# A two-layer transformer on one core: moving work between stages, normalisations to ScalarE, and a later load

## The chip, the cores and the metric

The kernel runs on one core of a Trainium2 chip. The core has five engines that run side by side, each through its own list of instructions in order: TensorE (PE, matrix products into PSUM), VectorE (DVE), ScalarE (ACT), GpSimd (POOL) and SyncE (SP, which here only issues DMA transfers). An instruction waits at the head of its engine's list until semaphores reach given values, and all that stands behind it waits with it. The metric is the time of one execution on the device in microseconds; lower is better.

## The reference

`x` is one sequence of T = 2048 tokens with C = 256 features. Two layers follow one another, each attention and then an FFN, each with normalisation before and behind it:

```python
x = x + LN(attn0(LN(x)))      # low-rank projections, rotary halves of the heads
x = x + LN(ffn(LN(x)))
x = x + LN(attn1(LN(x)))      # one qkv projection
x = x + LN(ffn(LN(x)))

# attention 0, H = 16 heads of 16 (8 plain + 8 rotary features)
c_q  = LN85(x @ W_d_q.T + b) * g + b2         # 85 features
q    = c_q @ W_u_q.T + b                      # second half of each head rotated
c_kv = x @ W_d_kv.T + b                       # 128 features, LN128 as kv_n, and 8 for k_r
k_n, v = kv_n @ W_u_kv.T + b                  # k = [k_n, rotated k_r]
# both attentions
y = softmax(causal(q @ k.T * scale)) @ v      # T x T scores for each head
out = y @ W_o.T + b_o
# both FFNs, 256 -> 1024 -> 256, int8 weights with a scale for each column
silu(h @ w_gate * s_gate) * (h @ w_up * s_up) @ w_down * s_down
```

LN is (x - mean) / sqrt(var + eps) over the features.

## The kernel before

Tokens lie in 16 tiles of 128, or in 4 chunks of 512 (`NCH` = 4, `TPC` = 4 tiles in a chunk). One program holds both layers one behind the other. Each layer `L` has four stages.

**Projections.** Queries and keys are made in 16 units (`UNITS`), each one product of 128 rows by 512 tokens (`unit_products`, TensorE). Each unit is then split into three bf16 parts, so that scores can be made from bf16 products: `split_hi` (ScalarE, L519), `unit_rem` (VectorE, L681), `split_mid` (ScalarE, L524), `split_lo` (GpSimd, L423). SyncE stores the parts to HBM (L354), and reads them back as stacks, in which a head's parts stand in the order that the scores want: `load_queries` (L329) and `load_keys` (L340) take three DMAs each, of 3, 2 and 1 copies of 16 rows with 4 KB in a row. `load_stacks(g, c)` does both for head group `g` (4 heads) and chunk `c`; there is room for two groups, `g % 2`. Values are made in 8 steps (`v_products`, TensorE; `v_value`, VectorE, L688). In layer 0 the units need a down-projection first: `chunk_down` (VectorE, L735 to L744), a root on ScalarE (L549), `chunk_z` (VectorE, L754, eight normalising operations a chunk), a transpose (L961, L962), and L552 on ScalarE. The plans `PE_BEFORE`, `DVE_BEFORE` and `ACT_BEFORE` say before which unit each chunk of that is done.

**Attention.** 16 steps, each one head group and one chunk of queries, in the order `STEP_ORDER`: group 0 with chunks 0, 1, 2, 3 (steps 0 to 3), then group 1 with chunks 3, 2, 1, 0 (steps 4 to 7), and so on. The string `TURNS` sets by hand in which order TensorE takes S (a 128x512 or shorter piece of scores; VectorE takes its maximum, L780 or, on the diagonal, L782), M (the maxima become rows), T (transposed scores; ScalarE takes the exponential, L569), V (probabilities times values) and Y (end of a step). The other engines follow the same order. TensorE waits before the first S that uses a stack until it has landed (`stack_in`). Thirty-three pieces of scores stand before the first T, and the first T of step 2 is the T with number 24; the first S of step 4 is turn 221 and needs the stacks of group 1 for chunks 3 and 0.

The loads of group 1 are issued by SyncE in the order of chunks 0, 1, 2, 3, behind this wait (`s.t_filled` counts the T products; `T_N` is their number in a layer):

```python
                sp.wait_ge(s.t_filled, L * T_N + 1)
                for c in range(NCH):
                    load_stacks(1, c)
                for n, (g, Q) in enumerate(STEPS):
```

Before the first S of a layer, TensorE waits until all 16 units' `unit_rem` and all 8 values are done (`p.rem`, `p.v_sb`).

**Output projection.** 16 products with W_o, bias (VectorE, L817), normalisation (statistics L627 and L630, root L488 on ScalarE, `normalize_branch` L640 on VectorE, added to `x` by GpSimd, L428), and the normalisation of the sum for the FFN (`normalize_residual`, L664), transposed on TensorE (L882) and moved by `move_transposed` (L503) and `low_parts` (L672).

**FFN.** 32 iterations `u` = (chunk `c`, block `i` of 128 hidden features): eight gate and up products, silu (ScalarE, L603), the product of both (VectorE, L847), a low part (VectorE L850, GpSimd L472), and, one iteration late, twelve down products. The last of a chunk is taken out by VectorE (L838) and normalised as above for chunk `c - 1` while chunk `c` runs. Layer 1's transposes, units and values stand behind the last iteration of layer 0's FFN.

## Time and profile before

| | us |
|---|---|
| median of 3 executions | 1278.7 (1278.65 to 1279.92) |
| the profiled execution | 1275.28, of it 1273.5 in the span |
| projections, layer 0 | 0 to 86.0 |
| attention, layer 0 | 86.0 to 506.3 |
| output projection, layer 0 | 506.3 to 534.5 |
| FFN, layer 0 | 534.5 to 645.0 |
| projections and first scores, layer 1 | 645.0 to 723.5 |
| attention, layer 1, from its first T | 723.5 to 1126.6 |
| output projection, layer 1 | 1126.6 to 1154.8 |
| FFN, layer 1 | 1154.8 to 1263.9 |

TensorE is busy for 1164.4 us (91% of the span), VectorE for 1049.9, ScalarE for 720.6, GpSimd for 334.7. The rows of a window give the stretch, its length, the busy time and the number of instructions of each engine, the TensorE clock that was granted as a share of full speed, and the DMA engines' busy share and rate. The rows of a timeline give start, duration (of a run of like instructions), engine, line, what is written and read, the count, and in brackets how long the engine was idle before and what released it. A product of float32 stands in the trace as two records (pieces) of TensorE.

### The profile page before, as it was taken

The numbers are of one execution on the slowest core, as the hardware profiler recorded it, in microseconds if no ns is written. First come the engines' busy times: TensorE is split into PE (matmuls) and PEld (weight loads), VectorE is DVE, ScalarE is ACT, GpSimd is POOL, SyncE is SP. The second block draws the span as 40 slices with busy tenths as digits, with TensorE's granted clock in tenths as the row PEclk, the third lists the DMA queues.
The fourth block names the chain that finished last, engine by engine and source line by source line (L and its number), as shares of the span: only waits on it lengthen the run. The fifth ranks groups of instructions, "written<-read, shape, count | busy, mean of one in ns | idle before, by whom it ended". The sixth has DMA issues, their size and how long they took to land.

```text
span 1273.5 us, 35512 instructions
## 1 busy us (share of the span) xinstructions
PE 1164.4 (91%) x14872; PEld 586.6 (46%) x14872; DVE 1049.9 (82%) x2746; ACT 720.6 (57%) x919; POOL 334.7 (26%) x561
## 2 busy tenths in 40 slices
PE   5769999999999998799978789999999999987996
PEld 4432344544444543566645224455444445454664
DVE  7759999999999862878863899999999988558776
ACT  2441377767677886234342407777767778843332
POOL 2321211122111133433442212111231112424433
PEclk9976699999999999899999659999999999997998
DMA  5354000211100000000026320021120000000000
GB/s 173 121 160 109 25 15 15 64 28 37 43 3 2 3 4 3 18 16 1 1 77 190 85 87 15 15 56 28 30 58 4 3 3 3 4 1 2 17 18 33
DMA packets 31600, 49.95 MB, mean 39 GB/s; under 512 B 7245, under 2 KB 24143, under 8 KB 31431
## 3 DMA queue, kind: packets, MB, share of 16 engines
q1 hardware_dynamic: 25376, 41.95, 11.9%
q0 software_dynamic: 5488, 5.34, 1.4%
q8 instruction: 117, 1.92, 0.6%
q10 hardware_dynamic: 576, 0.39, 0.1%
q14 instruction: 43, 0.35, 0.1%
HBM read 32.56 MB, written 14.68 MB: 37 GB/s over the span
## 4 chain that ended last, share of the span: by engine, by line
PE 68%; DVE 19%; DMA 4%; ACT 3%; POOL 3%; issue 2%; SPq 1%; ACTq 0%; POOLq 0%; DVEq 0%
PE ps L887 65%; DVE m_tile L780 6%; DVE ps L782 3%; DMA k_parts<-parts 2%; DVE region_p L640 1%; DVE stats L627 1%; ACT region_p L569 1%; DMA q_parts<-parts 1%; PE ps L1034 1%; POOL q_stack L455 1%; DVE region_p L838 1%; PE ps L882 1%; DVE rem L681 1%; POOL parts L423 1%; DVE region_p L754 1%
## 5 line engine op out<-in xcount | busy, mean ns | idle before, releaser
L569 ACT ACTIVATE region_p<-ps 128x1024 f32<-128x1024 f32 (+3 forms) x640 | 541.4, 894 | 246.9 <-PE ps L887 243.4
L780 DVE TENSOR_REDUCE m_tile<-ps 128x1 f32<-128x512 f32 x768 | 501.3, 685 | 28.0 <-PE ps L887 22.5
L887 PE MATMUL ps<-k_stack,q_stack 96*32 96x512 bf16 (+3 forms) x5120 | 435.2, 375 | 21.4 <-DVE v_all L688 7.6
L887 PE MATMUL ps<-q_stack,k_stack 99*32 99x512 bf16 (+3 forms) x5120 | 350.5, 352 | 3.6 <-ACT region_p L569 2.2
L887 PE MATMUL ps<-region_p,v_all 128*17 128x512 f32 (+3 forms) x2560 | 292.8, 531 | 5.0 <-POOL region_p L460 4.8
L782 DVE CUSTOM_DVE_ANT_0 ps<-ps,causal 128x128 f32<-128x128 f32 (+3 forms) x512 | 248.7, 497 | 27.8 <-PE ps L887 26.3
L887 PEld LDWEIGHTS ps<-k_stack,q_stack 96*32 96x32 bf16 x5120 | 144.0, 96 | 256.5 <-DVE m_tile L780 104.0
L887 PEld LDWEIGHTS ps<-q_stack,k_stack 99*32 99x32 bf16 x5120 | 140.3, 98 | 153.3 <-issue 56.7
L460 POOL TENSOR_SCALAR_AFFINE_SELECT region_p<-region_p 128x512 f32<-128x512 f32 x128 | 81.1, 635 | 275.3 <-ACT region_p L569 269.7
L887 PE MATMUL ps<-region_a,w_ffn 128*128 128x512 f16 x512 | 125.8, 392 | 6.1 <-DVE region_a L672 5.2
L603 ACT ACTIVATE k_stack<-ps,cols 128x512 f32<-128x512 f32 x64 | 44.0, 688 | 129.9 <-PE ps L887 125.2
L472 POOL TENSOR_TENSOR y_chunk<-k_stack 128x512 bf16<-128x512 f32 x64 | 66.9, 1046 | 121.6 <-DVE k_stack L850 121.6
L455 POOL DMA_DIRECT2D q_stack<-m_rows x128 | 70.0, 553 | 107.4 <-DVE m_rows L796 104.3
L887 PEld LDWEIGHTS ps<-region_p,v_all 128*17 128x17 f32 x2560 | 70.8, 98 | 49.9 <-POOL region_p L460 9.6
L887 PE MATMUL ps<-w_ffn,k_stack 128*128 128x256 bf16 x512 | 87.4, 273 | 2.8 <-POOL y_chunk L472 2.8
L847 DVE SCALAR_TENSOR_TENSOR k_stack<-ps,cols,k_stack 128x512 f32<-128x512 f32 x64 | 47.4, 741 | 41.8 <-ACT k_stack L603 39.5
L887 PEld LDWEIGHTS ps<-region_a,w_ffn 128*128 128x128 bf16 x512 | 51.2, 100 | 59.0 <-issue 13.1
L442 POOL CAST m_parts<-neg_max 128x16 bf16<-128x16 f32 x32 | 6.3, 196 | 262.0 <-DVE neg_max L789 262.0
L782 DVE DVE_READ_ACCUMULATOR2_ANT m_tile<- 128x1 f32 x512 | 72.1, 141 | 0.0
L887 PE MATMUL ps<-w_ffn,y_chunk 128*128 128x256 bf16 x256 | 69.8, 273 | 0.0
L681 DVE SCALAR_TENSOR_TENSOR rem<-ps,cols,parts 128x512 f32<-128x512 f32 x32 | 23.7, 747 | 50.7 <-ACT parts L519 40.7
L423 POOL TENSOR_TENSOR parts<-rem,parts 128x512 bf16<-128x512 f32 x32 | 36.4, 1154 | 97.4 <-ACT parts L524 97.4
(93 smaller groups left out, 895.6 us busy)
## 6 DMA issues: line engine op xcount, KB each, us to landing
k_parts<-parts SPq DMA_DIRECT2D x16, 384.0 KB, 7.9
q_parts<-parts SPq DMA_DIRECT2D x16, 384.0 KB, 8.7
q_stack<-q_parts SPq DMA_DIRECT2D x32, 192.0 KB
k_stack<-k_parts SPq DMA_DIRECT2D x32, 192.0 KB
q_stack<-q_parts SPq DMA_DIRECT2D x32, 128.0 KB
k_stack<-k_parts SPq DMA_DIRECT2D x32, 128.0 KB
X<-in_x SPq DMA_DIRECT2D x4, 512.0 KB, 6.6
q_stack<-q_parts SPq DMA_DIRECT2D x32, 64.0 KB
```

What stands on the lines that cost most here:

```text
L423: nc.gpsimd.tensor_tensor(parts[:, u % PB, 2, :], rem[:, u % 2, :], parts[:, u % PB, 1, :], ALU.subtract).then_inc(proj[L].lo, 1)
L455: pool.dma_start(dst, src).then_inc(mrows_in[o.n % 2], 16)
L460: nc.gpsimd.affine_select(out=blk, in_=blk, compare_op=ALU.is_ge, fill=0.0, base=0, pattern=[[0, HG], [1, P]], channel_multiplier=-1).then ...
L472: nc.gpsimd.tensor_tensor(flo_r[:, u % 3, :], frem_r[:, u % 3, :], frem_hi[:, u % 3, :], ALU.subtract).then_inc(ffn[L].lo, 1)
L569: nc.scalar.activation(probs[:, o.j % SLOTS, 2 * o.hp:2 * o.hp + 2, o.off:CH], psT[:, o.k % 2, :, o.off:CH], ACT.Exp, scale=SCALE).then_in ...
L603: nc.scalar.activation(gate_r[:, u % 2, :], ps[:, u % 2, :], ACT.Silu, scale=col("s_gate", layer=L, at=i)).then_inc(f.gate, 1)
L627: nc.vector.bn_stats(stats[:, i, which, :], tiles[:, i, :]).then_inc(after, 1)
L681: nc.vector.scalar_tensor_tensor(rem[:, u % 2, :], ps[:, u % 4, :], unit_bias(L, u), parts[:, u % PB, 0, :], ALU.add, ALU.subtract).then_i ...
L780: nc.vector.tensor_reduce(maximum, scores, AX.X, ALU.max).then_inc(s.ring_free, 1)
L782: nc.vector.tensor_tensor_reduce(scores, scores, causal[:, CH - n:CH], 1.0, MASKED, ALU.add, ALU.max, maximum).then_inc(s.ring_free, 1)
L847: nc.vector.scalar_tensor_tensor(fuse_r[:, u % 3, :], ps[:, 2 + u % 2, :], col("s_up", layer=L, at=i), gate_r[:, u % 2, :], ALU.mult, ALU. ...
L887: return pe.matmul(o, a, b, start=first, stop=last)
```

## The change

- **Layer 0's start.** Units 12 to 15 and the eight values are no longer made before the first S but between the first S pieces, at the turns that the tables `UNITS_AT`, `REM_AT`, `VALUES_AT` and `VALUES_SB_AT` name. What waited before the first S now waits before the first T.
- **Normalisations.** The normalising operations of L640, L664 and L754 go from VectorE to ScalarE, as `Identity` with a scale and a bias for each row; VectorE keeps a reciprocal and a small product for them (`inverse`).
- **Layer 1's projections.** Of layer 1, the transposes of chunks 0 to 2, units 0 to 11 and values 0 to 3 are threaded through the 32 iterations of layer 0's FFN (`early_jobs`, `side_jobs`), with their normalisations, splits and remainders; values 4 and 5 come right behind it; the last chunk's transposes, units 12 to 15 and values 6 and 7 stand between layer 1's first S pieces.
- **GpSimd.** A chunk's four additions to `x` come together behind iteration 3, where they came in pairs behind iterations 4 and 5.
- **SyncE.** In both layers the loads of group 1 wait for the first T of step 2 (the 25th T) where they waited for the layer's first T.

```diff
+    STEP2_T = min(o.k for o in ORDER if o.kind == "T" and o.n == 2)
...
-            [("qk", m, c) for c in range(NCH) for m in (0, 2)] + [("qk", m, c) for c in range(NCH) for m in (1, 3)],
+            [("qk", m, c) for c in range(NCH) for m in (0, 2, 1, 3)],
...
+        def chunk_ready(L, u):
+
+            if L == 0:
+                return (u - 1) // 3 - 1 if u % 3 == 1 and 4 <= u <= 13 else None
+            return u // 4 if u % 4 == 3 else None
+
+        def chunk_units(L, c):
+            return 3 * (c + 1) if L == 0 else 4 * c + 2
...
-        DVE_BEFORE = {0: [("down", 0), ("down", 1), ("z", 0)], 1: [("down", 2), ("c", 0), ("z", 1)],
-                      3: [("down", 3)], 4: [("c", 1), ("z", 2)], 7: [("c", 2), ("z", 3)], 10: [("c", 3)]}
-        ACT_BEFORE = {0: [("sqrt", 0), ("sqrt", 1)], 1: [("c", 0), ("sqrt", 2)], 3: [("sqrt", 3)], 4: [("c", 1)],
-                      7: [("c", 2)], 10: [("c", 3)]}
+        DVE_BEFORE = {0: [("down", 0), ("z", 0), ("down", 1), ("z", 1)], 1: [("down", 2), ("c", 0), ("z", 2)],
+                      3: [("down", 3), ("z", 3)], 4: [("c", 1)], 7: [("c", 2)], 10: [("c", 3)]}
+        ACT_BEFORE = {0: [("sqrt", 0), ("z", 0), ("sqrt", 1), ("z", 1)], 1: [("c", 0), ("sqrt", 2), ("z", 2)],
+                      3: [("sqrt", 3), ("z", 3)], 4: [("c", 1)], 7: [("c", 2)], 10: [("c", 3)]}
...
+        def early_jobs(u):
+
+            jobs = []
+            for d in range(NCH - 1):
+                i = u - NI * (d + 1)
+                late = 1 if d < NCH - 2 else 0
+                jobs += [(job, d) for job, at in (("branch", 2), ("stats", 4), ("norm", 4 + late), ("x", 5 + late),
+                                                  ("pair0", 6 + late), ("pair1", 7 + late), ("rest", 8 + late)) if at == i]
...
+        def side_jobs(L, u):
+
+            c, i = divmod(u, NI)
+            jobs = [("x16", 2 * c + 2), ("x16", 2 * c + 3)] if u < NCH * NI and i == XHAT_AT[c] + 2 else []
+            for job, d in early_jobs(u) if L == 0 else []:
+                if job == "x":
+                    jobs += [("x", 2 * d), ("x", 2 * d + 1)]
+                if job in ("pair0", "pair1"):
+                    first = 4 * d + 2 * (job == "pair1")
+                    jobs += [("unit", first), ("unit", first + 1)]
+                if job == "rest":
+                    jobs += [("v", 2 * d), ("v", 2 * d + 1)]
+            return jobs
+
...
+        UNITS_AT = ({2: 12, 4: 13, 6: 14, 8: 15}, {8: 12, 10: 13, 12: 14, 14: 15})
+        REM_AT = ({4: 12, 6: 13, 8: 14, 10: 15}, {10: 12, 12: 13, 14: 14, 16: 15})
+        VALUES_AT = ({10: 0, 12: 1, 14: 2, 16: 3, 18: 4, 20: 5, 22: 6, 24: 7}, {16: 6, 18: 7})
+        VALUES_SB_AT = ({12: 0, 14: 1, 16: 2, 18: 3, 20: 4, 22: 5, 24: 6, 26: 7}, {18: 6, 20: 7})
+        LOW_AT = ({}, {15: (12, 13), 16: (14, 15)})
+        assert FIRST_T > max(max(at) for at in VALUES_SB_AT)
...
-                sp.wait_ge(s.t_filled, L * T_N + 1)
+                sp.wait_ge(s.t_filled, L * T_N + STEP2_T + 1)
...
-                    if i in (4, 5) and c > 0:
-                        for t in range(2):
-                            add_residual(2 + 2 * L, TPC * (c - 1) + 2 * (i - 4) + t)
+                    if i == 3 and c > 0:
+                        for t in range(TPC):
+                            add_residual(2 + 2 * L, TPC * (c - 1) + t)
...
+            def normalize_branch(k, b):
+
+                act.wait_ge(turn[k].rstd_done, 2 * (b + 1))
+                for i in range(TPC * b, TPC * (b + 1)):
+                    nc.scalar.activation(A[:, i, :], A[:, i, :], ACT.Identity, scale=rstd[:, i, 0:1],
+                                         bias=nbias[:, i, 0:1]).then_inc(turn[k].normed, 1)
...
+                    elif what == "z":
+                        act.wait_ge(p.rstd, 2 * (c + 1))
+                        for i in range(TPC * c, TPC * (c + 1)):
+                            for w, cs in ((0, slice(0, DQ)), (1, slice(DQ, DQ + DKV))):
+                                nc.scalar.activation(c_down[:, i, cs], c_down[:, i, cs], ACT.Identity,
+                                                     scale=rstd[:, i, w:w + 1], bias=nbias[:, i, w:w + 1]
+                                                     ).then_inc(p.z, 1)
...
+                normalize_branch(k1, 0)
...
+                    if i == 3 and c > 0:
+                        normalize_branch(k2, c - 1)
+                    if i == XHAT_AT[c] + 1:
+                        normalize_residual(k1, c + 1)
+                    for job, d in early_jobs(u) if L == 0 else []:
+                        if job == "x":
+                            normalize_residual(2, d)
...
+                    for job, d in early_jobs(u) if L == 0 else []:
+                        if job == "norm":
+                            sqrt_residual(2, d)
+                        if job == "x":
+                            move_transposed(2, d)
+                        if job == "pair0":
+                            split_hi(1, 4 * d)
+                            split_hi(1, 4 * d + 1)
+                            split_mid(1, 4 * d)
+                        if job == "pair1":
+                            split_hi(1, 4 * d + 2)
+                            split_mid(1, 4 * d + 1)
+                            split_hi(1, 4 * d + 3)
+                            split_mid(1, 4 * d + 2)
...
-            def normalize_branch(k, b):
-
-                tn = turn[k]
-                bs = slice(TPC * b, TPC * (b + 1))
-                dve.wait_ge(tn.std_done, b + 1)
-                nc.vector.reciprocal(rstd[:, bs, 0], std[:, bs, 0]).then_inc(tn.rstd_done, 1)
-                dve.wait_ge(tn.rstd_done, b + 1)
-                for i in range(TPC * b, TPC * (b + 1)):
-                    nc.vector.tensor_scalar(A[:, i, :], A[:, i, :], mv[:, i, 0, 0:1], rstd[:, i, 0:1], ALU.subtract,
-                                            ALU.mult).then_inc(tn.normed, 1)
+            def inverse(tn_done, bs, w, at):
+
+                nc.vector.reciprocal(rstd[:, bs, w], std[:, bs, w]).then_inc(tn_done, 1)
+                dve.wait_ge(tn_done, 2 * at + 1)
+                nc.vector.scalar_tensor_tensor(nbias[:, bs, w], mv[:, bs, w, 0], -1.0, rstd[:, bs, w], ALU.mult,
+                                               ALU.mult).then_inc(tn_done, 1)
...
+                for at, o in enumerate(ORDER):
+                    if at in REM_AT[L]:
+                        unit_rem(L, REM_AT[L][at])
+                    if at in VALUES_SB_AT[L]:
+                        v_value(L, VALUES_SB_AT[L][at])
...
+                        if job == "stats":
+                            stats_residual(2, d)
+                        if job == "norm":
+                            inverse_residual(2, d)
+                        if job in ("pair0", "pair1"):
+                            first = 4 * d + 2 * (job == "pair1")
+                            unit_rem(1, first)
+                            unit_rem(1, first + 1)
+                        if job == "rest":
+                            v_value(1, 2 * d)
+                            v_value(1, 2 * d + 1)
...
+            def side(L, kind, n):
+
+                j = SIDE[L].index((kind, n))
+                if j >= 2:
+                    pe.wait_ge(*side_release(L, *SIDE[L][j - 2]))
+                if kind == "x16":
+                    transpose_pair(1 + 2 * L, n)
+                elif kind == "x":
+                    transpose_pair(2, n)
+                elif kind == "unit":
+                    unit_products(1, n)
+                else:
+                    v_products(1, n)
...
+                    for u in range(EARLY):
+                        for what, c in PE_BEFORE.get(u, []):
+                            chunk_tensor(what, c)
+                        unit_products(0, u)
...
+                    if L == 1 and at == X_AT:
+                        transpose_batch(2, NCH - 1)
+                    if at in UNITS_AT[L]:
+                        unit_products(L, UNITS_AT[L][at])
+                    if at in VALUES_AT[L]:
+                        v_products(L, VALUES_AT[L][at])
+                    if at == FIRST_T:
+                        pe.wait_ge(p.rem, NU)
+                        pe.wait_ge(p.v_sb, VU)
...
-                    if i == XHAT_AT[c] + 2:
-                        transpose_batch(k1, c + 1)
+                    for kind, n in side_jobs(L, u):
+                        side(L, kind, n)
```

TensorE where layer 0 goes from its last units to the first scores, before (`q_stack,w_attn` of 512 is a unit, `w_attn,q_stack` of 256 two values, `k_stack,q_stack` a piece of scores):

```order
L887 MATMUL ps<-q_stack,w_attn 128x512 x3
L887 MATMUL ps<-w_attn,q_stack 128x256 x4
L887 MATMUL ps<-q_stack,w_attn 128x512
L887 MATMUL ps<-w_attn,q_stack 128x256 x4
L887 MATMUL ps<-q_stack,w_attn 128x512
L887 MATMUL ps<-w_attn,q_stack 128x256 x4
L887 MATMUL ps<-q_stack,w_attn 128x512
L887 MATMUL ps<-w_attn,q_stack 128x256 x4
L887 MATMUL ps<-k_stack,q_stack 32x128 x4
L887 MATMUL ps<-k_stack,q_stack 32x256 x4
L887 MATMUL ps<-k_stack,q_stack 32x384 x4
```

and after:

```order
L1030 MATMUL ps<-q_stack,w_attn 128x512 x2
L1030 MATMUL ps<-k_stack,q_stack 32x128 x4
L1030 MATMUL ps<-k_stack,q_stack 32x256 x4
L1030 MATMUL ps<-q_stack,w_attn 128x512
L1030 MATMUL ps<-k_stack,q_stack 32x384 x4
L1030 MATMUL ps<-k_stack,q_stack 32x512 x4
L1030 MATMUL ps<-q_stack,w_attn 128x512
L1030 MATMUL ps<-k_stack,q_stack 32x128 x4
L1030 MATMUL ps<-k_stack,q_stack 32x256 x4
L1030 MATMUL ps<-q_stack,w_attn 128x512
```

Scores stand between units 13, 14 and 15, and the values have moved further down among the scores.

ScalarE in layer 0's projections, before (`std` is a root, `parts` a unit's first part):

```order
L549 ACTIVATE std<-mv,eps 128x8 x2
L519 ACTIVATE parts<-ps,cols 128x512
L552 ACTIVATE q_stack<-ps,cols 85x512
L549 ACTIVATE std<-mv,eps 128x8
L519 ACTIVATE parts<-ps,cols 128x512
L524 CAST parts<-rem 128x512
L519 ACTIVATE parts<-ps,cols 128x512
```

and after (ahead of these rows the same block of a root and eight operations stands once more):

```order
L643 ACTIVATE std<-mv,eps 128x8
L648 ACTIVATE region_p<-region_p,nbias,rstd 128x85
L648 ACTIVATE region_p<-region_p,nbias,rstd 128x128
L648 ACTIVATE region_p<-region_p,nbias,rstd 128x85
L648 ACTIVATE region_p<-region_p,nbias,rstd 128x128
L648 ACTIVATE region_p<-region_p,nbias,rstd 128x85
L648 ACTIVATE region_p<-region_p,nbias,rstd 128x128
L648 ACTIVATE region_p<-region_p,nbias,rstd 128x85
L648 ACTIVATE region_p<-region_p,nbias,rstd 128x128
L612 ACTIVATE parts<-ps,cols 128x512
```

Each root now has eight normalising operations behind it, and the first unit's part comes behind two such blocks.

ScalarE in layer 0's FFN, in chunk 1, before (`k_stack<-ps` is silu, L488 and L494 are roots, L503 moves transposed tiles):

```order
L488 ACT_TABLE_LOAD
L488 ACTIVATE std<-mv,eps 128x4
L603 ACT_TABLE_LOAD
L603 ACTIVATE k_stack<-ps,cols 128x512 x2
L505 CAST region_a<-ps 128x2x256 x2
L603 ACTIVATE k_stack<-ps,cols 128x512 x6
L494 ACT_TABLE_LOAD
```

and after, from the same root on (L576 and L583 normalise, L717 is silu, L598 moves):

```order
L563 ACT_TABLE_LOAD
L563 ACTIVATE std<-mv,eps 128x4
L576 ACTIVATE region_p<-region_p,nbias,rstd 128x256 x4
L717 ACT_TABLE_LOAD
L717 ACTIVATE k_stack<-ps,cols 128x512
L583 ACTIVATE region_p<-X,nbias,rstd 128x256 x4
L717 ACTIVATE k_stack<-ps,cols 128x512 x2
L598 CAST region_a<-ps 128x2x256 x2
L569 ACT_TABLE_LOAD
L569 ACTIVATE std<-mv,eps 128x4
L583 ACTIVATE region_p<-X,nbias,rstd 128x256 x4
L717 ACT_TABLE_LOAD
```

Behind the first root stand four normalising operations, four more come two iterations later, and a second switch of tables with a root and four more operations is new: there layer 1's first chunk is normalised. Further on, layer 1's units are split between the silu operations.

## Rows read from the trace of the kernel before

**Rows 1.** Windows by stage: length, busy us by engine, granted clock, DMA share, GB/s
```profile
86.00:506.30 420.30, 407.11 (x6488) 178.81 (x6488) 371.25 (x960) 285.06 (x341) 89.13 (x193) 0.94 0.12 29
...
506.30:534.50 28.20, 18.95 (x96) 15.93 (x96) 23.01 (x79) 9.26 (x17) 8.91 (x12) 0.91 0.00 1
...
534.50:645.00 110.50, 105.74 (x672) 65.54 (x673) 88.95 (x198) 39.04 (x56) 48.53 (x53) 0.98 0.04 11
...
645.00:723.50 78.50, 61.49 (x291) 31.84 (x293) 42.59 (x127) 29.75 (x46) 21.74 (x25) 0.87 0.41 131
```

**Rows 2.** Timeline of SyncE's queue: start, us, engine, line, out<-in, count
```profile
102.52 1.85 SPq L329 DMA_DIRECT2D q_stack<-q_parts  x3
...
121.13 1.58 SPq L340 DMA_DIRECT2D k_stack<-k_parts  x3
...
742.85 1.91 SPq L340 DMA_DIRECT2D k_stack<-k_parts  x3
```

**Rows 3.** Windows after the loads for head group 1, columns as in rows 1
```profile
129.00:132.00 3.00, 3.00 (x24) 0.56 (x20) 3.00 (x9) 0.00 (x0) 0.00 (x0) 0.50 0.13 51
...
138.00:141.00 3.00, 2.65 (x24) 0.62 (x24) 2.97 (x10) 0.00 (x0) 2.01 (x7) 0.50 0.10 41
...
141.00:144.00 3.00, 2.84 (x28) 0.63 (x28) 3.00 (x7) 0.00 (x0) 1.01 (x2) 0.50 0.04 7
```

**Rows 4.** Timeline of TensorE and VectorE, brackets give idle before and its releaser
```profile
161.47 0.62 PE L887 MATMUL ps<-q_stack,k_stack 99*32 99x512 bf16 x8 [0.41 <-DMA q_stack<-m_rows]
...
178.74 1.88 DVE L780 TENSOR_REDUCE m_tile<-ps 128x1 f32<-128x512 f32 x3
...
782.32 0.61 PE L887 MATMUL ps<-q_stack,k_stack 99*32 99x512 bf16 x8
...
799.72 1.88 DVE L780 TENSOR_REDUCE m_tile<-ps 128x1 f32<-128x512 f32 x3
```

**Rows 5.** Timeline of SyncE's queue where one chunk is loaded alone
```profile
265.10 1.84 SPq L329 DMA_DIRECT2D q_stack<-q_parts  x3
```

**Rows 6.** Windows behind that load, columns as in rows 1
```profile
276.00:278.00 2.00, 2.00 (x48) 1.06 (x44) 2.00 (x5) 1.61 (x3) 1.77 (x6) 1.00 0.02 4
```

**Rows 7.** Window behind an idle stretch, columns as in rows 1
```profile
534.50:540.40 5.90, 5.87 (x16) 2.21 (x17) 3.70 (x7) 0.69 (x1) 4.07 (x6) 0.57 0.20 47
```

**Rows 8.** One line's instructions: count, min/median/max ns, first and last start, form
```profile
L552 ACT ACTIVATE q_stack<-ps,cols x4: 771/774/775, 36.0 to 59.6; 85x512 f32<-85x512 f32 x4
```

**Rows 9.** Timeline of VectorE and ScalarE in the first layer's projections
```profile
32.91 0.66 DVE L735 TENSOR_TENSOR region_p<-ps,rows 128x213 f32<-128x213 f32 x2
...
36.24 0.36 DVE L744 BATCH_NORM_AGGREGATE mv<-stats 128x2 f32<-128x6 f32 x4
...
45.64 0.67 ACT L519 ACTIVATE parts<-ps,cols 128x512 bf16<-128x512 f32 x1
...
75.85 0.69 ACT L519 ACTIVATE parts<-ps,cols 128x512 bf16<-128x512 f32 x1 [7.16 <-DMA k_parts<-parts]
```

**Rows 10.** Timeline of TensorE from the output projection into the FFN
```profile
529.96 1.97 PE L882 MATMUL ps<-ident,region_p 128*128 128x128 f32 x8 [5.75 <-DVE region_p L664]
...
534.53 1.87 PE L887 MATMUL ps<-region_a,w_ffn 128*128 128x512 f16 x4 [2.61 <-DVE region_a L672]
```

**Rows 11.** Timeline of TensorE in the second layer's projections
```profile
645.03 1.91 PE L882 MATMUL ps<-ident,region_p 128*128 128x128 f32 x16
...
660.82 8.82 PE L887 MATMUL ps<-region_a,w_attn 128*128 128x512 f32 x20 [2.19 <-DVE rem L681]
...
691.03 1.99 PE L887 MATMUL ps<-w_attn,region_a 128*128 128x256 f32 x8
```

**Rows 12.** Timeline of ScalarE and TensorE inside the first layer's FFN
```profile
626.72 1.28 ACT L494 ACT_TABLE_LOAD   x1
...
568.85 0.59 PE L887 MATMUL ps<-w_ffn,zeros 1*128 1x512 bf16 x2 [0.67 <-DVE region_p L838]
```

**Rows 13.** Groups of instructions, FFN: line, engine, operation, count, busy us, mean ns, idle
```profile
L428 POOL TENSOR_TENSOR X<-X,region_p 128x256 f32<-128x256 f32 x16 | 12.3, 793 | 1.2 <-DVE region_p L640 1.2
```

243 lines of the change are left out of this document (142 added, 101 removed).

## The prediction

> **What bounds the kernel now.** I read the windows by stage first [rows 1]. In layer 0's attention TensorE is busy for 407 of 420.3 us, in the FFN for 105.7 of 110.5. There TensorE's own list is the time, and work added to it costs its full length. Two stages are different. From the attention's end to the FFN TensorE has 18.95 busy us in 28.2 and VectorE 23.0: a chain through VectorE. And from the FFN's end to layer 1's first T it has 61.5 in 78.5, part of it at a lower clock (0.87). So work threaded into the FFN must be paid there, and what it saves is the stretch of 78.5 us. Then I read SyncE's queue [rows 2] and the DMA windows behind it [rows 3], since the change delays a load, and the timelines where that load's data is first used [rows 4]. The sum is made against the profiled execution, 1275.28 us, which lies 3.4 under the median of 1278.7; 3.4 is added at the end.
>
> **The late load: the largest loss.** Before, group 1's stacks are issued from 102.52 on, in eight rows of three DMAs (first and last shown), the last at 121.13; in layer 1 the last is at 742.85 [rows 2]. One more row of three, queries for a later group, follows at once. Behind the last issue the DMA engines show a flat share of 0.13 at 51 GB/s, which is two of sixteen engines working, until the window of 138 to 141 (0.10) and a rest in the next (0.04 of 3 us, about 0.9 us at 0.13) [rows 3]. So the whole batch ends near 141.4, 39 us after its first issue. Group 1 is eight of its nine rows if queries and keys cost alike, four of five query rows if keys cost nothing: 34.7 or 31.2 us. I take 33.5, nearer to the first since keys do cost something. Where one chunk goes alone, it is issued at 265.10 and the engines are quiet (0.02) from 276 on, 11 us [rows 5, 6]; four of those in a row would be 44, so overlap matters and 38 is my upper bound.
>
> After, the load waits for the first T of step 2. It stands at 161.47 and lasts 0.62, so the issue comes at 162.1 [rows 4]. Chunk 3, the last to be issued, is what step 4 asks for first: its stacks land at 162.1 + 33.5 = 195.6. The first maximum of step 4 is at 178.74 [rows 4], its scores 0.5 earlier, at 178.2. TensorE's order between these points is not touched, so it stands at that S for 195.6 - 178.2 = 17.4 us, with every T and V that is queued behind it. ScalarE and VectorE hang on TensorE there, and nothing in the profile can fill it. Layer 1: T at 782.32, issue at 782.9, landing at 816.4, the scores due at 799.2 [rows 4]: 17.2. Behind an idle stretch TensorE is granted 0.57 for 5.9 us (the FFN's start) [rows 7], which costs 5.9 x 0.43 = 2.5 more. Together 20 in each layer, **+40**. Bounds per layer: 5 (a load of 20 us and little clock lost) to 25 (38 us).
>
> Keys move on few rows, queries are read three and two times over. The Trainium skill, "DMA: Bandwidth & Descriptors", section "Why a DMA increments its semaphore by 16 and not by 1", says that a DMA is spread over the largest number up to 16 that divides its pattern's outer dimension; by that a read of 3 copies goes to three engines and one of 2 to two, and the two busiest would carry 156 rows of 4 KB each for the four chunks. The trace agrees with two engines at the end [rows 3]. By its count, at 51 GB/s over two engines, the last chunk would land after about 28 us as an estimate, the stall would be 12 a layer, and the sum 12 lower.
>
> **Layer 0's start.** The eight normalising operations a chunk go to ScalarE, in front of the units' first parts. The nearest row is an activation with scale and bias for each row, 85x512, 774 ns [rows 8]; for 85 and 128 columns I take 0.33 us apiece, 2.7 a chunk. A chunk's down-projection costs VectorE 3.7 us (32.91 to 36.60) [rows 9]. Walked through in order, the first part of unit 3 comes at 53.3 where it came at 45.64 [rows 9]: root and z of chunk 3 must precede it, and they wait for VectorE's fourth down block, which waits behind remainders that wait for ScalarE. That is +7.5, and stores and loads of the first stacks move with it. Against it: ScalarE waits 7.16 us for stored parts before unit 13 [rows 9], and six to nine scores are now worked off in that wait, minus the value steps (1.99 a piece [rows 11]) that now stand between the scores: -2.5. **+5**, bounds -3 (all of the wait is used) to +9.
>
> **Output projection to FFN.** The last normalisations stand in front of TensorE: idle 5.75 until 529.96 and 2.61 until 534.53, both for VectorE [rows 10]. Eight operations of normalising less on VectorE, done on a ScalarE that is busy for 9.3 of 28.2 us [rows 1], let the FFN start near 530.6: **-4** in each layer, **-8**, bounds -2 and -6.5 a layer.
>
> **Layer 0's FFN.** TensorE's list grows by 24 transposes at 0.12 (1.91 for 16 [rows 11]) = 2.9; 12 units at 1.76 (8.82 for five [rows 11]) = 21.2; four values at 1.9 (1.99 [rows 11]) = 7.6. Sum 31.7. Nothing hides that, TensorE being busy 96% [rows 1]. Then waits: a table load is 1.28 us [rows 12] and the change adds three pairs; four normalising operations are about 2 us; GpSimd's four additions, now together, 4 x 0.79 = 3.2 [rows 13] ahead of its low parts. I take 1.4 at each chunk boundary and up to 5 in all where transposes wait for ScalarE, less about 1.3 that each boundary spends now (0.67 seen at 568.85 [rows 12]): +7. **+38.7**, bounds 29 (the stage's own waits filled by the new products) to 50 (ScalarE late in every iteration with side work).
>
> The Trainium skill, "ScalarE: Activation LUTs", section "What ACT_TABLE_LOAD costs", puts a switch at 1283 ns and a drain of 1380 ns. The trace shows the load alone, 1.28 [rows 12], with the root right behind it. With the drain each pair would be about 5.3 as an estimate, and three more pairs would move the FFN up by some 10.
>
> **Between FFN and layer 1's first T.** Now 78.5 us [rows 1]. After the change there remain the last chunk's chain (the batch that now ends in the stall until 660.82 takes 15.8 [rows 11], in part under first scores), four units 7.0, four values 7.6, and 33 scores, for which VectorE's maxima need about 15. Some scores lie in the chain. I take 43: **-35.5**, bounds -30 and -40. What it saves is the other side of the FFN's 38.7: the products keep their length, only 10 to 15 us of waits and low clock are won, and three quarters of them are lost again to waits of the FFN.
>
> **Layer 1's FFN** has the normalisations on ScalarE and no side work: +2, bounds -3 and +6. The rest of the program keeps its order.
>
> **Sum.** 40 + 5 - 8 + 38.7 - 35.5 + 2 = +42.2; 1275.3 + 42.2 = 1317.5, as a median 1320.9, said as 1320.
>
> **Rivals.** (A) The load lands in time. If the four chunks of group 1 need less than 17 us from the issue, there is no stall at all and the two losses of 20 go: 1320 - 40 = 1280, and with a start or an FFN 5 us better than my terms, 1275: not slower. For it: in the new place no other group's transfers are under way. Against it: the drain lasts 19 us after its last issue is done, and one chunk alone took 11 [rows 2, 3, 6]. Chance 0.10, from the point of 17 us on. (B) The threading is better hidden than I have it (FFN +30, seam -40, start 0): 1304. For it: the FFN's waits come in pieces of 1 to 3 us that a product could fill; against it: these are waits for the same engines that get the side work. 0.13. (C) ScalarE falls behind in the FFN, with silu, splits, moves and normalisations on one list: its 39 busy us of 110 [rows 1] become about 39 + 12 x 1.3 + 28 x 0.55 + 8 = 78, which has room on the mean but not near a chunk's boundary; if each of three chunks loses 5 more: 1336. 0.09. That the change doesn't do what it says has no case of its own: the order of instructions shows it.
>
> **How the numbers follow.** Forecast 0.68, its own range 1308 to 1332. The range of 1292 to 1340 takes in B, C and a shorter stall (10 a layer); it leaves out A and the tails. A measurement can tell about 0.2% (2.6 us) from no change. Slower 0.91: forecast, B, C and the tail of A that stays above 1281.3. Same 0.03, faster 0.06, from A with good terms.
>
> **What would show it.** Late load: TensorE idle for about 17 us at step 4's first S in each layer, released by a DMA into the stacks, and a granted clock near 0.57 behind it; if less than 3, rival A. Start: first T of layer 0 about 5 us later. FFN: 149 us long, with gaps at chunk boundaries before the down products; more than 160 is C. Seam: 43 us from the last down product to the first T. FFN's start 4 us sooner after the attention. Wrong would be, above all, a load that is not paced by two engines.

## The result, and the profile after the change

The changed kernel takes 1343.9 us (median of 4 executions, 1343.6 to 1346.7) where the kernel before takes 1278.7: a ratio of 1.051, 95% interval 1.050 to 1.053. It is slower, as forecast, by 65 us where 41 were forecast, and 1343.9 lies above the range's end of 1340. The profiled execution took 1343.64 us, its span is 1341.9.

The windows of the changed kernel by stage (columns as in rows 1) answer to [rows 1]: layer 0's attention from its first scores, output projection, FFN of layer 0, from its last product to layer 1's first T, and FFN of layer 1.

```profile
76.23:537.60 461.37, 425.99 (x6528) 188.82 (x6528) 381.25 (x982) 293.89 (x354) 96.60 (x199) 0.91 0.13 35
...
537.60:564.56 26.96, 20.98 (x97) 16.29 (x97) 16.61 (x68) 16.28 (x35) 8.73 (x13) 0.88 0.00 1
...
564.56:721.49 156.93, 143.49 (x776) 83.62 (x777) 86.86 (x192) 83.17 (x132) 57.97 (x62) 0.95 0.14 42
...
721.49:767.01 45.52, 30.24 (x187) 13.41 (x186) 28.71 (x98) 18.47 (x25) 10.83 (x18) 0.72 0.38 109
...
1216.68:1331.95 115.27, 106.41 (x672) 64.42 (x672) 70.39 (x142) 52.14 (x81) 44.65 (x48) 0.99 0.04 14
```

The output projection went from 28.2 to 27.0, layer 0's FFN from 110.5 to 156.9, the stretch behind it from 78.5 to 45.5, layer 1's FFN from 109.1 (1154.8 to 1263.9 in the table of the kernel before) to 115.3. In the attention TensorE was busy for 407 of 420 us and now is for 426 of 461: 35 us without work where 13 were.

The first row below is SyncE's first load for group 1, the others are TensorE at step 4's first scores in layer 0 and layer 1; the bracket is the idle time before.

```profile
174.84 1.40 SPq L391 DMA_DIRECT2D q_stack<-q_parts  x2
...
208.23 1.04 PE L1030 MATMUL ps<-k_stack,q_stack 96*32 96x512 bf16 x8 [17.23 <-issue]
...
860.88 1.04 PE L1030 MATMUL ps<-k_stack,q_stack 96*32 96x512 bf16 x8 [17.04 <-issue]
```

These answer to [rows 2, 4]. The issue now stands at 174.84 and the scores that need the last stack start at 208.23, 33.4 us later, behind 17.23 us of idle time; 17.04 in layer 1. The releaser is printed as "issue", which means that the profile shows no semaphore event for it. That it is the load, the runs below show. Two windows of the DMA engines lie inside this load, and one at its end:

```profile
178.00:182.00 4.00, 4.00 (x84) 2.00 (x84) 3.99 (x8) 3.02 (x6) 1.27 (x2) 1.00 0.93 166
...
190.90:208.20 17.30, 0.10 (x4) 0.00 (x1) 0.54 (x3) 0.35 (x1) 0.83 (x4) 0.64 0.28 91
...
207.00:208.20 1.20, 0.00 (x0) 0.00 (x1) 0.00 (x0) 0.00 (x0) 0.00 (x0) 0.50 0.13 48
```

Only the end shows the share of two engines of sixteen (0.13); before it the share is higher.

To set the two profiles side by side I counted TensorE's products of each kind (S, T, V in the order of `TURNS`, which the change doesn't touch; before the first T it has 32 pieces of scores and one M, not 33 pieces) and compared when the same product starts. Times are starts in TensorE's timeline, or differences of two.

| | before | after | longer by | forecast |
|---|---|---|---|---|
| first T of layer 0 | 101.4 | 111.5 | 10.1 | 5 |
| T 24 of layer 0 | 161.5 | 174.1 | 12.6 | 5 |
| T 24 to the last V of layer 0 | 341.2 | 359.7 | 18.5 | 20 |
| last V to the FFN's first product | 31.9 | 30.8 | -1.1 | -4 |
| layer 0's FFN, to its last down product | 110.4 | 156.8 | 46.4 | 38.7 |
| from there to layer 1's first T | 78.6 | 45.6 | -33.0 | -35.5 |
| first T to last V of layer 1 | 399.4 | 419.0 | 19.6 | 20 |
| last V to the FFN's first product | 31.9 | 30.7 | -1.2 | -4 |
| layer 1's FFN | 108.7 | 115.2 | 6.5 | 2 |
| sum (spans 1273.5 and 1341.9) | | | 68.4 | 42.2 |

So the forecast missed by 26 us, and not in one place: 7.6 at the start, 7.7 and 4.5 in the FFNs, 2.9 and 2.8 in the output projections, 2.5 behind layer 0's FFN; the stalls came out 1.9 smaller. The medians differ by 65.2 and the profiles by 68.4, since the profiled execution before was 3.4 faster than its median; its start is one likely part of that, see the last section.

### The profile page after: what moved, and what is told of

Its sections match the earlier page's. It is cut to its first block, busy times and chain, and to the rows that moved or that the text cites. A ratio compares the mean times of both kernels' runs of the same rounds, so it can differ in the third digit from the quotient of the medians.

```text
span 1341.9 us, 35575 instructions
## 1 busy us (share of the span) xinstructions
PE 1187.3 (88%) x14872; PEld 589.9 (44%) x14872; DVE 1000.7 (75%) x2634; ACT 796.0 (59%) x1069; POOL 332.0 (25%) x561
## 4 chain that ended last, share of the span: by engine, by line
PE 58%; DVE 17%; issue 10%; POOL 6%; ACT 5%; DMA 3%; SPq 0%; ACTq 0%; POOLq 0%; DVEq 0%
PE ps L1030 55%; DVE m_tile L910 7%; DVE ps L912 3%; POOL y_chunk L537 2%; DVE stats L756 2%; DMA k_parts<-parts 1%; DMA q_stack<-m_rows 1%; POOL q_stack L520 1%; ACT region_p L670 1%; PE ps L1200 1%; ACT region_p L583 1%; PE ps L1025 1%; DVE k_stack L977 1%; POOL X L490 1%; ACT region_p L576 1%
## 5 line engine op out<-in xcount | busy, mean ns | idle before, releaser
L537 POOL TENSOR_TENSOR y_chunk<-k_stack 128x512 bf16<-128x512 f32 x64 | 66.5, 1039 | 155.6 <-DVE k_stack L980 155.6
L717 ACT ACTIVATE k_stack<-ps,cols 128x512 f32<-128x512 f32 x64 | 43.0, 684 | 75.9 <-PE ps L1030 75.8
L1030 PEld LDWEIGHTS ps<-w_ffn,k_stack 128*128 128x128 bf16 x512 | 48.4, 98 | 26.0 <-POOL y_chunk L537 8.1
```

Source lines behind the costliest of these rows:

```text
L537: nc.gpsimd.tensor_tensor(flo_r[:, u % 3, :], frem_r[:, u % 3, :], frem_hi[:, u % 3, :], ALU.subtract).then_inc(ffn[L].lo, 1)
L717: nc.scalar.activation(gate_r[:, u % 2, :], ps[:, u % 2, :], ACT.Silu, scale=col("s_gate", layer=L, at=i)).then_inc(f.gate, 1)
L1030: return pe.matmul(o, a, b, start=first, stop=last)
```

## Experiments

All were run beside the kernel before on the same chip, whose medians there were 1276.2 to 1278.0. A time with an interval has 4 to 6 executions, the others have one; what single ones tell is read from their traces. The changed kernel was not run again beside them, so a difference of times to its 1343.9 carries 2 us or so of difference between chips. "The middle" is the way from layer 0's last V to layer 1's first T, 220.9 before and 233.2 after.

### The late load

The changed kernel with the load where it was:

```diff
-                sp.wait_ge(s.t_filled, L * T_N + STEP2_T + 1)
+                sp.wait_ge(s.t_filled, L * T_N + 1)
```

> The changed kernel with one edit: group 1's stacks are loaded behind the layer's first T again, as before the change. Theory, the load needs a fixed time: it took 33.4 us from its issue at 174.84 to the first product of step 4 at 208.23, and behind the first T (111.5) it lands near 145, long before step 4's first scores are due at 190.7. Both gaps of TensorE (17.2 us each) go, and the slow clock behind them: 1343.9 - 2 x 19 = 1306. Rival, the transfers move into a place where they disturb the first steps, so that only part comes back: 1320 or more. Rival, step 4 waits for something else that only ends at the same time: 1344.

Measured: 1305.3 us, ratio to before 1.022 (1.021 to 1.024): 38.6 less than 1343.9. From T 24 to the last V of layer 0 it takes 340.0 (359.7 in the changed kernel), from the first T to the last V of layer 1 400.0 (419.0): 38.7 together. TensorE at step 4 of layer 0 in this kernel:

```profile
193.81 1.03 PE L1030 MATMUL ps<-region_p,v_all 128*17 128x512 f32 x8
...
194.67 0.60 PE L1030 MATMUL ps<-k_stack,q_stack 96*32 96x512 bf16 x8
```

The scores at 194.67 follow the product ahead of them without idle time, and nothing of the gain is lost to the load in its old place.

The other way round, the kernel before with only the late load:

```diff
-                sp.wait_ge(s.t_filled, L * T_N + 1)
+                sp.wait_ge(s.t_filled, L * T_N + 24 + 1)
```

> The kernel before with one edit: group 1's stacks wait for the T with number 24. Theory: T 24 is at 161.5, landing 33.4 us after the issue at 162.1, scores of step 4 due at 178.2: a gap of 17.3 in each layer, and about 2 us of slow clock behind each: 1278.7 + 2 x 19 = 1317. Rival, the gap of the changed kernel belongs to its shifted start and its other edits: 1279 to 1295.

Measured: 1318.1 us, 1.031 (1.029 to 1.034), 42 us more than the kernel before on that chip; the two stretches with the stalls grew by 18.4 and 19.7, 38.1 together. Both stalls stand in it (TensorE, step 4 of layers 0 and 1):

```profile
199.72 1.04 PE L887 MATMUL ps<-k_stack,q_stack 96*32 96x512 bf16 x8 [17.06 <-issue]
...
841.73 1.04 PE L887 MATMUL ps<-k_stack,q_stack 96*32 96x512 bf16 x8 [16.95 <-issue]
```

The two runs agree: by the traces the late load is worth 38 to 39 of the 65 us, in the changed kernel and in the kernel before (by the times 39 and 42).

The same load, late, in another order:

```diff
-                for c in range(NCH):
-                    load_stacks(1, c)
+                load_queries(1, NCH - 1)
+                for c in range(NCH):
+                    load_keys(1, c)
+                for c in range(NCH - 1):
+                    load_queries(1, c)
```

> The changed kernel, with the same 24 DMAs of group 1 in another order at the same late place: the queries of chunk 3 and the keys of all four chunks first, then the other queries. Step 4's first row of scores needs just these. Theory, the DMAs are worked off one after the other at a fixed rate and a row of queries costs as much as a row of keys: five of eight rows are needed, 33.4 x 5/8 = 21 us, landing at 195.7 where 190.7 is due: a gap of 5 in each layer in place of 17.2, time about 1320. If keys cost nothing against queries, the gap is 0 (1307). Rival, all DMAs in flight share the engines and end together: gap near 17, 1344.

Measured: 1340.3 us, little less. My expectation was wrong by an oversight: queries and keys of a chunk count on one semaphore (`stack_in`), so the scores of a chunk wait for its queries too, which they don't read. TensorE in this kernel:

```profile
198.00 0.62 PE L1033 MATMUL ps<-k_stack,q_stack 96*32 96x512 bf16 x4 [6.88 <-DMA q_stack<-q_parts]
...
203.34 0.62 PE L1033 MATMUL ps<-k_stack,q_stack 96*32 96x512 bf16 x4 [4.72 <-DMA q_stack<-q_parts]
...
208.70 0.62 PE L1033 MATMUL ps<-k_stack,q_stack 96*32 96x512 bf16 x4 [3.88 <-DMA q_stack<-q_parts]
```

The first scores came 10 us sooner, and then each next chunk of keys was let go 5.4 us later than the last, when its queries had landed; the 15.5 us of idle time are nearly the 17.2 of before. It does show how long a chunk's queries take: 5.35 us. Four times that is 21.4 of the load's 33.4 us; the other 12 fall to the keys and the start. Whether keys first would pay with semaphores of their own was not tried.

### The start of layer 0

Normalising of the down-projection back on VectorE (`chunk_z` as in the kernel before), the changed plans kept:

```diff
-                        inverse(p.rstd, bs, slice(0, 2), c)
+                        nc.vector.reciprocal(rstd[:, bs, :], std[:, bs, :]).then_inc(p.rstd, 1)
+                        dve.wait_ge(p.rstd, c + 1)
+                        for i in range(TPC * c, TPC * (c + 1)):
+                            for w, cs in halves:
+                                nc.vector.tensor_scalar(c_down[:, i, cs], c_down[:, i, cs], mv[:, i, w, 0:1],
+                                                        rstd[:, i, w:w + 1], ALU.subtract, ALU.mult).then_inc(p.z, 1)
```

> The changed kernel with one edit: in layer 0's projections the normalising operations of the down-projection are on VectorE again; order of chunks and units as changed. Theory, these operations in ScalarE's list delay the units' first parts: layer 0's first T comes 7 us sooner than 111.5, and the time is about 1337. Rival, the values and units between the first scores, at half the TensorE clock, cost what the start lost: the first T stays within 2 us of 111.5 and the time within 3 us of 1343.9.

Measured: 1341.4 us in one execution; the first T at 107.1. This execution ran its first 24 down products in 6.6 us, where the changed kernel's profile has 4.7; after_early_load, with the same start as the changed kernel, ran them in 7.0 and had its first T at 116.0. The expectation below calls this a matter of the granted clock; it is not, the clock reads 1.00 in all these traces from 22.5 to 30. Compared with after_early_load, normalising on VectorE brings the first T 8.9 us forward, 8.3 when both are counted from their first down product. The total tells less, as it is one execution, and its stall was 1.7 longer.

Units 12 to 15 and the values before the first scores again, normalising left on ScalarE:

```diff
-        UNITS_AT = ({2: 12, 4: 13, 6: 14, 8: 15}, {8: 12, 10: 13, 12: 14, 14: 15})
+        UNITS_AT = ({}, {8: 12, 10: 13, 12: 14, 14: 15})
...
+                    for u in range(EARLY, NU):
+                        unit_products(0, u)
+                        v_products(0, 2 * (u - EARLY))
+                        v_products(0, 2 * (u - EARLY) + 1)
+                    pe.wait_ge(p.v_sb, VU)
```

> The changed kernel, layer 0's units 12 to 15 and its eight values before the first scores again; normalising stays on ScalarE. The first T of layer 0 was at 101.4 before, at 111.5 changed, and, compared at a like granted clock in the first 30 us, 9 sooner with the down-projection's normalising on VectorE. Theory, the interleaving itself neither wins nor loses much (2 us): first T near 109 to 113. Rival, it did hide work and only the normalising cost time: first T at 117 or later.

Measured: 1343.3 us; first T at 114.1 (111.5 with the interleaving, both with the first down products in 4.7 us), T 24 at 175.1 (174.1). The interleaving wins 2.6 us at the first T, but only 1.0 are left at T 24. That is a little above the theory's 109 to 113 and below the rival's 117: the interleaving is not where the start's 10 us went.

### The stretch between FFN and layer 1's scores

TensorE of the changed kernel at layer 1's first scores and first T:

```profile
733.56 0.83 PE L1030 MATMUL ps<-k_stack,q_stack 96*32 96x128 bf16 x12 [8.45 <-DMA k_stack<-in_ones]
...
767.01 1.04 PE L1030 MATMUL ps<-q_stack,k_stack 99*32 99x512 bf16 x8 [3.65 <-DMA q_stack<-m_rows]
```

The wait of 8.45 us for the rows of ones was no part of my sum; before, it was hidden by the units. Moved to the first T:

```diff
-                else:
-                    pe.wait_ge(ones_in, 48)
...
                     if at == FIRST_T:
+                        if L == 1:
+                            pe.wait_ge(ones_in, 48)
                         pe.wait_ge(p.rem, NU)
```

> The changed kernel; TensorE's wait for the rows of ones in layer 1, which now stands before the first scores (8.45 us idle until 733.56), moved to the first T. Theory, only these rows hold the scores up: the first scores come 7 to 8 us sooner, the first T 6 us sooner than 767.0, time 1338. Rival, behind it the wait for VectorE to take out the last chunk's down products, or the last chunk's own chain, is nearly as late: the first T moves by less than 2 us, 1343.

Measured: 1344.6 us. The way from the last V to the first scores fell from 199.8 to 193.3, and the middle from 233.2 only to 232.7. The rival holds: something behind the wait is nearly as late; by the order of work it is the last chunk's own chain. A wait of 8.45 us in the trace was worth 0.5.

### Normalising on ScalarE, and the threading

All normalising of output projections and FFNs back on VectorE (`inverse` followed there by the four operations), threading kept:

```diff
-                inverse(turn[k].rstd_done, slice(TPC * b, TPC * (b + 1)), 0, b)
+                nc.vector.reciprocal(rstd[:, bs, 0], std[:, bs, 0]).then_inc(tn.rstd_done, 1)
+                dve.wait_ge(tn.rstd_done, b + 1)
+                for i in range(TPC * b, TPC * (b + 1)):
+                    nc.vector.tensor_scalar(A[:, i, :], A[:, i, :], mv[:, i, 0, 0:1], rstd[:, i, 0:1], ALU.subtract,
+                                            ALU.mult).then_inc(tn.normed, 1)
```

> The changed kernel with the normalising operations of both output projections and both FFNs back on VectorE, at the places where VectorE now makes the reciprocal; the threading stays, and so does the late load. Before, the stretch from the last product of layer 1's attention to the end took 150.6 us, changed 155.8; from layer 0's last to layer 1's first T 220.8 and 233.2. Theory, the moved operations make these stretches longer, through waits of transposes for ScalarE (9.0 us in layer 0's FFN) and the low clock behind them: 151 at the end, 226 in the middle, time 1332. Rival, the waits come from where the transposes stand in TensorE's order, whichever engine normalises: both stretches within 2 us of the changed ones, 1342.

Measured: 1327.6 us. The window of layer 0's FFN in it:

```profile
571.30:710.30 139.00, 135.57 (x779) 82.99 (x778) 98.59 (x219) 64.39 (x92) 55.80 (x57) 0.99 0.16 48
```

The FFN takes 139.0 against 156.8, at a clock of 0.99 against 0.95, and layer 1's 107.6 against 115.2. The middle fell to 218.3, below the 220.9 of the kernel before. It has two parts that go different ways. FFN and the stretch behind it take 139.0 + 44.6 = 183.6, against 189.0 before and 202.4 in the changed kernel: with VectorE normalising the threading wins 5.4 us, and ScalarE's normalising costs 18.8. The output projections went up to 34.7 and 36.0 (30.8 on ScalarE). In the changed order ScalarE is the better place there; the kernel before, with VectorE normalising in its own order, had 31.9.

Without the threading (`early_jobs` gives its jobs behind iteration 31, on every engine), normalising on ScalarE:

```diff
-                i = u - NI * (d + 1)
+                i = u - NCH * NI - 3 * d
```

> The changed kernel without the threading: layer 1's transposes, units 0 to 11 and values 0 to 5 stand behind the last FFN iteration of layer 0 on every engine (in the changed order of units); the last four units and two values stay between the first scores. Theory, the threading loses: the FFN falls from 157 to about 116 us, the stretch behind it grows from 45.5 to about 82, so that the way from layer 0's last attention product to layer 1's first T takes 225 us in place of 233.2; time 1336. Rival, the threading wins as it was counted on in the prediction's sum of parts at full clock, and the loss comes from elsewhere: 240 us or more, 1351.

Measured: 1348.3 us. Layer 0's FFN 115.8 as expected, but 88.3 from there to the first T where I had 82; the middle is 233.5, the same as with the threading. So neither branch: with ScalarE normalising, FFN and the stretch behind it take 204.1 without the threading and 202.4 with it, a gain of 1.7 where it is 5.4 with VectorE normalising. Of the total's 4.4 above the changed kernel, 4.1 lie ahead of the first T (115.6), which this edit doesn't touch.

Why is ScalarE's normalising so dear? ScalarE in layer 1's FFN of the changed kernel, where nothing is threaded, at a chunk's boundary:

```profile
1249.96 0.69 ACT L717 ACTIVATE k_stack<-ps,cols 128x512 f32<-128x512 f32 x1 [2.35 <-PE ps L1030]
...
1250.67 1.28 ACT L563 ACT_TABLE_LOAD   x1
...
1252.08 0.30 ACT L563 ACTIVATE std<-mv,eps 128x4 f32<-128x4 f32 x1
...
1254.57 2.07 ACT L576 ACTIVATE region_p<-region_p,nbias,rstd 128x256 f32<-128x256 f32 x4 [2.20 <-DVE nbias L765]
...
1256.66 1.28 ACT L717 ACT_TABLE_LOAD   x1
...
1257.96 0.69 ACT L717 ACTIVATE k_stack<-ps,cols 128x512 f32<-128x512 f32 x1
```

Silu, table load, root, then 2.20 us idle for VectorE's reciprocal and product (L765), four operations in 2.07, table load, silu: 8 us from one silu to the next where an iteration takes 3.03. The product takes its place on VectorE behind that iteration's own work, and the silu waits behind the normalising in ScalarE's list. The other block of the boundary (L583) waits 2.7 us in the same way. Part of both waits is VectorE's product itself: it takes 1.01 us here where others take 0.16, and ends just behind an instruction of GpSimd's (last section). Two experiments, both in layer 1's FFN alone. One block of the two at each boundary put behind the next silu:

```diff
-                    if i == 3 and c > 0:
+                    if i == 3 + L and c > 0:
                         normalize_branch(k2, c - 1)
```

(and the same for GpSimd's four additions.)

> The changed kernel; in layer 1's FFN alone, ScalarE takes the four operations of each finished chunk's normalising one silu later, and GpSimd its additions behind the next low part. Each time ScalarE stood idle 2.2 us (1254.57) for VectorE's small product, with the next silu behind it. Theory, this round trip at the head of ScalarE's list is what costs, not the length of the operations: three waits go, layer 1's FFN falls from 115.2 to 109 or 110. Rival, the length of the operations and the table loads cost: 114 or more.

Measured: 1336.6 us, layer 1's FFN 108.4 where it was 115.2. ScalarE at the same boundary:

```profile
1250.35 1.28 ACT L563 ACT_TABLE_LOAD   x1
...
1251.76 0.30 ACT L563 ACTIVATE std<-mv,eps 128x4 f32<-128x4 f32 x1
...
1252.08 1.28 ACT L717 ACT_TABLE_LOAD   x1
...
1254.05 0.69 ACT L717 ACTIVATE k_stack<-ps,cols 128x512 f32<-128x512 f32 x1 [0.69 <-PE ps L1030]
...
1254.64 2.06 ACT L576 ACTIVATE region_p<-region_p,nbias,rstd 128x256 f32<-128x256 f32 x4
```

The second table load now follows the root at once, the silu comes at 1254.05, and the four operations behind it start without waiting. 6.8 us are given back, all that was lost, with every operation still on ScalarE. The edit moves the wait and the block's 2.07 us together, so it doesn't tell the two apart.

Then the other chunk's four operations each done twice (the first time into unused space), with no wait added:

```diff
                 for i in range(TPC * b, TPC * (b + 1)):
+                    if k == 3 and b > 0:
+                        nc.scalar.activation(q_flat[:, 2048 + i * C:2048 + (i + 1) * C], X[:, i, :], ACT.Identity,
+                                             scale=rstd[:, i, 1:2], bias=nbias[:, i, 1:2])
```

> The changed kernel; in layer 1's FFN alone, each operation that normalises the next chunk's input runs twice on ScalarE, the first time into unused space: three blocks of 4 x 0.52 = 2.07 us more on ScalarE, with no wait added. The result is the same. Theory (round trips cost, not length): layer 1's FFN grows by less than 2 us from 115.2. Rival, ScalarE's time at a chunk's boundary is the bound: it grows by 3 x 2.07 = 6 us.

Measured: 1354.1 us, the FFN 125.0: 9.8 us more for 6.2 us of work. My theory in that form fell. Length costs as well, once the boundary is full: the round trip and the blocks stand in one row ahead of the silus, and here each further microsecond was paid with 1.6. The two runs together point to the place, ahead of a silu that is due, as what turns all of it into loss.

In both FFNs, every block behind its iteration's silu:

```diff
-                    if i == 3 and c > 0:
-                        normalize_branch(k2, c - 1)
-                    if i == XHAT_AT[c] + 1:
-                        normalize_residual(k1, c + 1)
...
                                          scale=col("s_gate", layer=L, at=i)).then_inc(f.gate, 1)
+                    if i == 3 and c > 0:
+                        normalize_branch(k2, c - 1)
+                    if i == XHAT_AT[c] + 1:
+                        normalize_residual(k1, c + 1)
```

(and the same for layer 1's first chunks, `normalize_residual(2, d)`.)

> The changed kernel; in both FFNs every block of four normalising operations stands behind the silu of its iteration on ScalarE instead of ahead of it, so that the silu doesn't wait for VectorE's reciprocal and small product. All operations stay on ScalarE. Theory (the round trip at the head of ScalarE's list is what the prediction left out): layer 1's FFN falls from 115.2 to about 108.5, as with the one block moved, and layer 0's from 156.8 to 140 to 145, near the 139.0 that it takes with the normalising on VectorE; time 1321 to 1326. Rival, in layer 0 the transposes that stand right behind the normalising in TensorE's order keep the waits: 150 or more there, 1331 or more.

Measured: 1324.2 us in one execution. Layer 1's FFN 106.8, less than before the change (108.7); layer 0's 147.5, between theory and rival. Of the 17.8 us that ScalarE's normalising costs in layer 0's FFN, 9.3 were the silu's waiting. First the waits of the changed kernel in layer 0's FFN (engine, line waited for, us in total, times, longest), two of ScalarE's and one of TensorE's:

```profile
ACT region_p L583 <- DVE nbias L765: 13.6, 6, 2.7
...
ACT region_p L576 <- DVE nbias L765: 4.3, 3, 2.2
...
PE ps L1025 <- ACT region_p L583: 9.0, 3, 3.9
```

and the same of this kernel:

```profile
ACT region_p L583 <- DVE nbias L765: 0.8, 1, 0.8
...
PE ps L1025 <- ACT region_p L583: 6.6, 3, 2.9
```

ScalarE's 17.9 us of waiting for VectorE's products became 0.8. TensorE's 9.0 of waiting for ScalarE ahead of the threaded transposes (L1025) became only 6.6: these stand right behind the normalising in TensorE's order, wherever the silu is. They are most of what is left of the 8.5 us to VectorE's 139.0; the clock (0.96 in this FFN, 0.99 there) may be the rest, which no run separates.

### Versions made of the good parts

Load early, normalising on VectorE in layer 0's projections and the FFNs, on ScalarE in the output projections, threading kept; with units and values ahead of the scores:

> The changed kernel with the parts undone that the runs so far show to cost: group 1's load behind the first T again, normalising in layer 0's projections and in both FFNs on VectorE, layer 0's units and values before the first scores. Left of the change: the threading and the output projections' normalising on ScalarE. From the segments of the runs so far: start as before (101 to 105 to the first T); output projection 30 us (before 31.9); FFN of layer 0 139.0, then 44.6 to the first T (before 110.4 and 78.6, so 5.4 less); layer 1's FFN 107.6 (before 108.7); sum 10 below the kernel before, 1266, ratio 0.992. Rival, the output projection's gain and the threading's gain don't add up, since the FFN's first waits move: 1272 to 1278.

Measured: 1272.0 us, 0.9964 (0.995 to 0.9978) of the kernel before. The FFNs (140.1, 106.8) and output projections (29.4) came as expected; the first T at 108.5 did not: its sum is spent in the start. So 1272 is in the rival's range, but not by the rival's cause. With the interleaving:

> As best_units_first, but with layer 0's last four units and its values between the first scores as in the change. With the normalising on VectorE the first T came 2.4 us later and T 24 3.5 us later than in the kernel before at a like clock (107.1 to 104.7, 169.3 to 165.8). Theory, it costs 2 to 4 us: 1269. Rival, these differences came from the state of the first 30 us: within 1 us of the other, or sooner.

Measured: 1270.0 us, 0.9946 (0.9934 to 0.9958). It is not slower than the other, so the theory fell and the rival held (the two intervals overlap). Both have normalising on VectorE as the kernel before has, and still a later first T. What is left is the order of the plans, which the change rewrote too:

```diff
-        DVE_BEFORE = {0: [("down", 0), ("z", 0), ("down", 1), ("z", 1)], 1: [("down", 2), ("c", 0), ("z", 2)],
-                      3: [("down", 3), ("z", 3)], 4: [("c", 1)], 7: [("c", 2)], 10: [("c", 3)]}
+        DVE_BEFORE = {0: [("down", 0), ("down", 1), ("z", 0)], 1: [("down", 2), ("c", 0), ("z", 1)],
+                      3: [("down", 3)], 4: [("c", 1), ("z", 2)], 7: [("c", 2), ("z", 3)], 10: [("c", 3)]}
```

> best_interleaved with the plans DVE_BEFORE and ACT_BEFORE of the kernel before, so that VectorE takes the second chunk's down-projection ahead of the first chunk's normalising again. With the changed plans and normalising on VectorE the first T came at 106.8 to 108.5, in the kernel before at 101.4 and 104.7. Theory, the order of the plans costs 3 to 4 us of the start's 10: first T at 103 to 104, ratio to the kernel before 0.992 where best_interleaved had 0.9946. Rival, the interleaving costs it: first T stays at 106 or later, 0.9946.

Measured: 1265.8 us, 0.9907 (0.9892 to 0.9921). The first T of layer 0 in best_interleaved and in this kernel:

```profile
106.84 0.62 PE L1050 MATMUL ps<-q_stack,k_stack 99*32 99x512 bf16 x4 [0.77 <-DMA q_stack<-m_rows]
...
98.67 0.62 PE L1050 MATMUL ps<-q_stack,k_stack 99*32 99x512 bf16 x4 [0.75 <-DMA q_stack<-m_rows]
```

8.1 us sooner. 1.2 of them lie ahead of the first down product (22.8 and 21.6), so in these two traces the order of a plan is worth 7, twice what I expected. The profiled execution was the fastest of its five, 3.9 below their median; by the ratios the order is worth 5. The first T is now 2.7 us ahead of the kernel before (101.4, with its first down product at 21.8), T 24 1.1: so much the interleaving wins. Two windows of this kernel, layer 0's FFN and from there to layer 1's first T, show the threading at its price:

```profile
530.00:669.00 139.00, 135.49 (x777) 82.51 (x776) 98.47 (x219) 66.01 (x95) 58.43 (x62) 0.99 0.16 47
...
669.00:713.20 44.20, 28.60 (x190) 13.29 (x189) 30.72 (x104) 14.34 (x17) 10.76 (x17) 0.78 0.39 111
```

139.0 + 44.2 = 183.2, against 110.5 + 78.5 = 189.0 [rows 1].

One more version put ScalarE's normalising behind the silu into best_interleaved, in place of VectorE's:

> best_interleaved (0.9946 of the kernel before), with the FFNs' normalising on ScalarE behind the silu instead of on VectorE. Theory: VectorE is relieved and the silu doesn't wait, FFNs of 107 and 138 us, 1266 to 1270. Rival, the transposes of layer 0's FFN still wait for ScalarE: 1275 or more.

Measured: 1282.2 us, 1.0041 (1.0025 to 1.0057), a little slower (six executions from 1279.7 to 1286.3, of which the profile is the longest). The rival held: layer 0's FFN takes 150.1 where VectorE's normalising takes 138.7.

## Why the prediction was right and wrong

**The late load, right.** 33.5 us from issue to landing were forecast, 33.4 lie between the issue and the scores that wait; 17.4 and 17.2 us of stall, 17.2 and 17.0. The choice near the upper bound (keys cost something) was right. The slow clock behind it was right too; the window behind the stall in the changed kernel:

```profile
208.20:214.00 5.80, 5.77 (x64) 2.42 (x68) 3.02 (x7) 2.07 (x3) 0.00 (x0) 0.61 0.14 57
```

0.61 for 5.8 us costs 2.3, where 2.5 were forecast from [rows 7]. Rival A is refuted. By the count of the Trainium skill, "DMA: Bandwidth & Descriptors", section "Why a DMA increments its semaphore by 16 and not by 1", the estimate was 28 us. Measured were 33.4, and 5.35 for a chunk's queries alone. So the batch is longer than two engines at 51 GB/s make it by that count, and the rows of the trace were the better guide. The prediction named as its main sign of being wrong a load that is not paced by two engines. The windows above show that share only at the load's end, and a mean share can't tell whether the two busiest engines pace it ahead of that. So the length was right because it was read from the same load in the kernel before; what paces it is not shown. In the kernel before, too, the flat share begins at 129, behind the last issue of the row that follows (122.76 to 127.64), and not behind 121.13.

**Layer 0's start: right cause, wrong sum.** Forecast +5, measured +10.1 at the first T and +12.6 at T 24. The step that failed is the walk through the new order. ScalarE in the start of the changed kernel:

```profile
27.48 0.30 ACT L643 ACTIVATE std<-mv,eps 128x8 f32<-128x8 f32 x1 [4.98 <-DVE mv L877]
...
28.25 3.04 ACT L648 ACTIVATE region_p<-region_p,nbias,rstd 128x85 f32<-128x85 f32 x8 [0.47 <-DVE nbias L765]
...
31.87 0.30 ACT L643 ACTIVATE std<-mv,eps 128x8 f32<-128x8 f32 x1 [0.57 <-DVE mv L877]
...
32.64 3.04 ACT L648 ACTIVATE region_p<-region_p,nbias,rstd 128x85 f32<-128x85 f32 x8 [0.47 <-DVE nbias L765]
...
35.59 0.66 ACT L612 ACTIVATE parts<-ps,cols 128x512 bf16<-128x512 f32 x1
...
56.14 0.67 ACT L612 ACTIVATE parts<-ps,cols 128x512 bf16<-128x512 f32 x1
```

Each block of eight takes 3.04 us, not 2.7, and has a wait of 0.47 for VectorE ahead. The first part of unit 3 comes at 56.14; I had 53.3, and 45.64 stood before [rows 9]. The change also put the normalising of a chunk ahead of the next chunk's down-projection in both plans, which I took for part of the move. Four profiles whose first 24 down products all take 4.7 us, and which differ by one step each up to the first T, separate the terms. Times count from the first down product:

| | first T | T 24 |
|---|---|---|
| before | 79.6 | 139.7 |
| with the interleaving (best_plan_before) | 77.0 | 138.8 |
| and the changed plans (best_interleaved) | 84.0 | 146.3 |
| and the normalising on ScalarE (after) | 88.9 | 151.5 |

So the interleaving is worth -2.6 at the first T, as forecast (-2.5), the order of the plans 7.0 and the move to ScalarE 4.9: 11.9 where I had 7.5 for both. The remaining 0.9 of the 10.1 is a later first down product (22.65 against 21.77), which lies between 21.6 and 23.4 in the traces here, whatever the kernel. In profiles whose first products take 6.6 to 7.0 us the split is another: 4.6 for the order (best_units_first against before_late_load) and 8.3 for the move (after_early_load against after_z_vector). Traces with the same program up to the first T, and the same pace, differ by up to 1.2.

**Output projections: -4 forecast, -1.1 and -1.2 measured.** I moved eight operations off VectorE and took their length as won. The first half came: the transposes start 25.2 us behind the last V where they started 27.3 behind it. The second half did not. TensorE's transposes and ScalarE in the changed kernel, then ScalarE in the kernel before, whose transposes start at 529.96 [rows 10]:

```profile
559.05 1.92 PE L1025 MATMUL ps<-ident,region_p 128*128 128x128 f32 x8 [1.13 <-ACT region_p L583]
...
560.38 2.06 ACT L576 ACTIVATE region_p<-region_p,nbias,rstd 128x256 f32<-128x256 f32 x4
...
562.53 1.04 ACT L598 CAST region_a<-ps 128x512 f16<-128x512 f32 x2
```

```profile
531.11 0.59 ACT L505 CAST region_a<-ps 128x512 f16<-128x512 f32 x1 [1.38 <-PE ps L882]
```

ScalarE moves the transposed tiles 3.5 us behind the start of the transposes where it was 1.15, since the next chunk's four normalising operations now stand ahead of that move in its list. ScalarE had room on the mean, but not in this place. The traces of after_early_load, after_keys_first and after_z_vector, with the same normalising, had 29.4, 2.5 less than before, which is still short of 4; why there are two values, no run shows.

**Layer 0's FFN: the term that was mis-sized most.** 31.7 us of TensorE's own work were right to a few us; with VectorE normalising the FFN grew by 28.6. To that I added 7 for waits; 17.8 were there (156.8 against 139.0 with VectorE normalising). The failed step is "four normalising operations are about 2 us". They are 2.07, but I priced ScalarE's blocks by their length and left out the round trip ahead of each: ScalarE makes the root, VectorE the reciprocal and the product behind its own work for that iteration, and ScalarE waits with the next silu queued behind. For the late load I had named what is queued behind the waiting instruction; for this wait I did not. It came to 17.9 us of idle time on ScalarE in layer 0's FFN, and made layer 1's FFN 6.5 us longer where I had 2. Rival C had the direction (ScalarE late at a chunk's boundary, 5 us for each of three chunks) but for the wrong reason, ScalarE's load. It got 0.09; its 1336 was the nearest number, but its own sign, an FFN of more than 160, did not come: that it was nearest is luck.

The Trainium skill, "ScalarE: Activation LUTs", section "What ACT_TABLE_LOAD costs", would have made the FFN some 10 us longer by its drain, as an estimate (three more pairs with two drains each are 8.3). The rows at 1250.67 and 1252.08 show the load of 1.28 and the root 0.13 behind its end, so that drain is not seen here. That the FFN did come out longer has the other cause, which moving the blocks shows.

**Behind the FFN:** -35.5 forecast, -33.0 measured. The wait for the ones was missed, but moving it won only 0.5, so it isn't what is missing.

**The range** was too narrow on the slow side. My bounds for each term were the bounds of that term's row, and the terms for the start, both FFNs and the output projections erred to the same side. In large part they rest on one assumption, that an operation moved to an idler engine costs its length, wherever it stands in that engine's list. Terms that share an assumption don't even out. (Rival B's own terms add up to 1303, not 1304.)

## What to carry to other kernels

Moving a step to an idler engine costs its length only if its inputs are ready when it reaches the head of the list; where they come from another engine that is in step with this one, put the step behind the next item that others wait for. A load that was early for no visible reason may be early because it takes as long as the distance to its use: measure issue to landing before moving it. And when an order of tables is rewritten along with a move, price both: here the order alone cost 5 to 7 us, and undoing it, the late load and the normalising on ScalarE outside the output projections turned a kernel of 1.051 into one of 0.991.

## What was unexpected in the hardware

The first 24 down products of layer 0 run at a fast or a slow pace, whatever the kernel; TensorE in the profiled execution before, and in before_late_load, where the program is the same up to there:

```profile
21.77 4.74 PE L887 MATMUL ps<-w_attn,region_a 128*128 128x213 f32 x24 [0.77 <-ACT region_a L503]
...
22.51 6.88 PE L887 MATMUL ps<-w_attn,region_a 128*128 128x213 f32 x24 [0.77 <-ACT region_a L503]
```

4.74 or 6.88 us, with the first T 3.3 us later in the second (104.7 to 101.4). Ten of the seventeen profiles have 4.74 or 4.75, the others 6.3 to 7.0; after and after_early_load, again one program up to there, have one of each. The granted clock reads 1.00 in all of them from 22.5 to 30, so it doesn't tell the two apart, and the cause stays open. The profile before had the short one. That may be part of the 3.4 us between its time and the median, which I added as a constant; the profile of the changed kernel has the short one too and lies only 0.2 below its median.

VectorE's product for the bias, a few numbers in each partition, has very different durations (count, then min, median and max in ns):

```profile
L765 DVE SCALAR_TENSOR_TENSOR nbias<-mv,rstd x32: 162/167/1016, 28.1 to 1335.8; 128x4 f32<-128x4 f32 x28, 128x8 f32<-128x8 f32 x4
```

Many take 0.16 us, others 1.02. At the FFN's boundary shown above, VectorE's timeline has a long one in the round trip, and GpSimd's has this beside it:

```profile
1253.32 0.17 DVE L763 RECIPROCAL rstd<-std 128x4 f32<-128x4 f32 x1
...
1253.52 1.01 DVE L765 SCALAR_TENSOR_TENSOR nbias<-mv,rstd 128x4 f32<-128x4 f32 x1
...
1253.48 1.04 POOL L537 TENSOR_TENSOR y_chunk<-k_stack 128x512 bf16<-128x512 f32 x1 [3.24 <-DVE k_stack L980]
```

GpSimd's low part (L537, 1.04 us) began 0.04 us ahead of the product and ended at 1254.52; the product ended at 1254.54. So it is in the whole trace: each of the 14 products that take more than 0.2 us started while a GpSimd instruction was under way and ended about 0.02 us behind that one's end, and none of the 18 short ones started so. The reciprocals ahead of them (L763) don't show this: six start while such an instruction is under way and take 0.17 to 0.18 us, like the rest. The products held up in this way are six in each FFN, 0.6 to 0.85 us apiece: about 5 us, as an estimate from these durations, of the 14.6 us that ScalarE waits for them in layer 1's FFN. No run moved GpSimd's work away from them, so what that would win is not shown.
